# Two head attentions with VectorE in another order and the normalisation cut in pieces; a gated expert layer with a 128-row spreading product and its splits ahead of the router

## What is computed

```python
scores = einsum(q, k) * inv_sqrt_d + mask          # layer 0, softmax, times v
topv, topi = top_k(softmax(t @ gate_w.T), 6)       # layer 2
cw = zeros((T, 16)).at[rows, topi].add(topv / sum(topv))
routed = einsum('eti,edi,te->td', silu(g) * u, ed_w, cw)
```

## Time and profile before

| | |
|---|---|
| median of 3 runs | 4728.63 us (4726.76 to 4732.03) |
| profiled execution | 4728.14 us |
| its span, first to last instruction | 4726.4 us |
| mean granted TensorE clock | 0.937 of full |
| PE / DVE / ACT / POOL busy | 4134.5 (87%) / 2611.0 (55%) / 2047.8 (43%) / 888.4 (19%) us |

### The profile page before, as it was taken

How to read it: one execution, slowest core, us unless ns; L and a number is a source line. 1 busy time by engine, 2 the same in 40 slices (tenths; PEclk the granted TensorE clock), 3 DMA queues, 4 the chain that set the end, 5 groups by cost and what they waited for, 6 DMA issues and landing times. The chain is left out here.

```text
span 4726.4 us, 74274 instructions
## 1 busy us (share of the span) xinstructions
PE 4134.5 (87%) x25324; PEld 3338.8 (71%) x25324; DVE 2611.0 (55%) x5915; ACT 2047.8 (43%) x5270; POOL 888.4 (19%) x714
## 2 busy tenths in 40 slices
PE   5886999999896876999999996999979997887791
PEld 3554899999775764878877885777767775665671
DVE  5876998989475336444444443433333333776533
ACT  4775666666222433434333433333333332665140
POOL 1001333323000330000000000222212222000145
PEclk9987999999997997999999997999989999998596
DMA  2001000000001003000000001000010000000244
GB/s 62 14 14 46 1 0 0 0 0 1 25 20 43 1 29 111 8 6 6 6 6 6 6 5 57 13 5 9 5 53 10 9 10 21 14 11 25 89 135 129
DMA packets 100269, 119.29 MB, mean 25 GB/s; under 512 B 13777, under 2 KB 81201, under 8 KB 99761
## 3 DMA queue, kind: packets, MB, share of 16 engines
q1 hardware_dynamic: 93152, 97.25, 6.5%
q0 software_dynamic: 6864, 18.75, 1.4%
HBM read 93.03 MB, written 22.94 MB: 25 GB/s over the span
## 5 line engine op out<-in xcount | busy, mean ns | idle before, releaser
L1145 ACT ACTIVATE peer_tab<-peer_sims 128x128 f32<-128x128 f32 x1024 | 305.6, 392 | 0.0
L1152 POOL TENSOR_TENSOR peer_tab<-peer_sims 128x2048 f32<-128x2048 f32 x64 | 244.7, 3843 | 289.9 <-ACT peer_sims L1129 260.7
L1200 DVE SCALAR_TENSOR_TENSOR peer_tab<-peer_tab,peer_th 128x2048 f32<-128x2048 f32 x128 | 294.9, 2345 | 0.3
L1217 PE MATMUL bank<-ident,peer_tab 128*128 128x128 f32 x2048 | 246.9, 274 | 20.0 <-DVE peer_tab L1200 20.0
L1217 PEld LDWEIGHTS bank<-ident,peer_tab 128*128 128x128 f32 x2048 | 233.7, 142 | 33.6 <-DVE peer_tab L1200 21.2
L1627 DVE COPY mha_ks<-bank 128x512 f32<-128x512 f32 x128 | 88.5, 691 | 302.0 <-PE bank L1592 299.5
L1267 PE MATMUL bank<-peer_wd,peer_hh 128*128 128x256 f32 x1024 | 242.1, 380 | 1.8 <-DVE peer_hh L1258 1.8
L1732 PE MATMUL bank<-mha_wo,mha_oT 128*128 128x256 f32 x1024 | 242.9, 380 | 0.0
L1240 PE MATMUL bank<-peer_hT,peer_wg 128*128 128x256 f32 x1024 | 241.9, 379 | 0.0
L643 DVE TENSOR_TENSOR moe2a_b<-moe2a_a,bank 128x512 f32<-128x512 f32 x104 | 71.5, 687 | 296.5 <-PE bank L556 273.7
L643 DVE TENSOR_TENSOR moe2b_b<-moe2b_a,bank 128x512 f32<-128x512 f32 x96 | 66.0, 687 | 273.3 <-PE bank L556 252.2
(11 more groups left out here) (518 smaller groups left out, 11105.8 us busy)
## 6 DMA issues: line engine op xcount, KB each, us to landing
m_y_rows<-moe_y SPq DMA_DIRECT2D x79, 128.0 KB, 1.7
att_ctxT<-in_ctxT_dram SPq DMA_DIRECT2D x32, 256.0 KB, 2.7
x<-in_x_dram SPq DMA_DIRECT2D x4, 1024.0 KB, 9.6
lin_ctxT<-in_ctxT_dram SPq DMA_DIRECT2D x16, 256.0 KB, 2.7
mem_ctxT<-in_ctxT_dram SPq DMA_DIRECT2D x16, 256.0 KB, 2.8
mem_ctx<-in_ctx_dram SPq DMA_DIRECT2D x16, 256.0 KB, 3.1
t_scratch<-mha_hTf SPq DMA_DIRECT2D x8, 512.0 KB, 4.8
moe2a_hTf<-t_scratch SPq DMA_DIRECT2D x8, 512.0 KB, 3.7
```

Source lines behind the costliest of these rows:

```text
L1145: i = nc.scalar.activation(tab[g][h][:, b * P:(b + 1) * P], sims[:, g, h, P:2 * P], ACT.Identity, bias=sims[:, g, h, b:b + 1])
L1152: nc.gpsimd.tensor_tensor(out=tab[g][h][:].rearrange("p (a b) -> p a b", b=P), in0=sims[:, g, h, P:2 * P].unsqueeze(1).broadcast_to([P, NB ...
L1200: nc.vector.scalar_tensor_tensor(out=tab[g][h][:], in0=tab[g][h][:], scalar=th[:, g, h:h + 1], in1=tab[g][h][:], op0=ALU.is_ge, op1=ALU.mu ...
L1217: i = nc.tensor.matmul(TB[n % 2][:, j * P:(j + 1) * P], tab[g][h][:, blk * P:(blk + 1) * P], core.ident[:], start=(j == 0 and h == 0), sto ...
```

## The change

In both head attentions VectorE's turn becomes one written-out order: residual of (t-2, 1), maxima of (t, 0), statistics of t+2, result of (t-1, 0), (layer 3: half of the spread keys, `square_dve`), result of (t-1, 1), residual of (t-1, 0), maxima of (t, 1), (layer 3: `neg_dve`), the rows of t+2, and the spread keys. `norm_dve` is cut into `stats_dve`, `square_dve` and `rows_dve`.

In the quantised stage `queries_dve` goes; ScalarE scales the queries by row (`queries_act`), and the scale by column and the bias are added when the transposed queries are copied (`q_copy`, two pieces). The mask is split into a high part (`mask_act`, ScalarE) and a rest (`mask_pool`, GpSimd), and the mask product becomes two fp32r products instead of one fp32 product. `columns_pe` and `columns_act` prepare the columns once.

In the expert layer `sel` and `cwT` get 128 rows, the lower 64 of them zero, so that the spreading product is a 128-row one. At the stage's start the splits of gate and up weights come ahead of the router, those of the down weights behind it, and TensorE waits for each only where it needs it.

```diff
-        sel, gw = sb("sel", [64, H], FP32R), sb("gw", [P, C, E])
+        sel, gw = sb("sel", [P, H], FP32R), sb("gw", [P, C, E])
...
-        cwTf, cwT_hi, cwT = sb("cwTf", [64, TILE]), sb("cwT_hi", [64, TILE], FP32R), sb("cwT", [64, 2, TILE], FP32R)
-        e_ready, cw_done, cw_zeroed, cw_init, cwTf_ready = sem("e_ready"), sem("cw_done"), sem("cw_zeroed"), sem("cw_init"), sem("cwTf_ready")
+        cwTf, cwT_hi, cwT = sb("cwTf", [64, TILE]), sb("cwT_hi", [64, TILE], FP32R), sb("cwT", [P, 2, TILE], FP32R)
+        e_ready, cw_done, cw_zeroed, cw_init, cwT_ready = sem("e_ready"), sem("cw_done"), sem("cw_zeroed"), sem("cw_init"), sem("cwT_ready")
+        sel_zeroed = sem("sel_zeroed")
...
+            act.wait_ge(cwT_ready, t)
         nc.scalar.activation(cwT[0:32, par, :], F[0:32, :], ACT.Copy)
+        if isinstance(t, int) and t < 2:
+            nc.scalar.activation(cwT[64:P, par, :], F[64:P, :], ACT.Copy)
...
-            pe.wait_ge(w_lo_made, (j // QB + 1) * (len(raws) - 1))
-            pe.wait_ge(w_hi_made, (j // QB + 1) * len(raws))
+            pe.wait_ge(w_lo_made, (j // QB) * (len(raws) - 1) + 2 * C)
+            pe.wait_ge(w_hi_made, (j // QB) * len(raws) + 2 * C)
...
+            if j == 0:
+                pe.wait_ge(cwT_ready, t + 1)
+            if is_first(t) and j % QB == 0:
+                pe.wait_ge(w_lo_made, (j // QB + 1) * (len(raws) - 1))
+                pe.wait_ge(w_hi_made, (j // QB + 1) * len(raws))
             nc.tensor.matmul(CW[:], sel[:, j * P:(j + 1) * P], cwT[:, par, :], start=True, stop=True).then_inc(cw_ready, 1)
...
-            nc.vector.tensor_tensor(out=cwT[32:64, par, :], in0=cwTf[32:64, :], in1=cwT_hi[32:64, :], op=ALU.subtract)
         nc.vector.tensor_tensor(out=hTs[1][:, par, :, :], in0=hTf[:], in1=hTs[0][:, par, :, :],
                                 op=ALU.subtract).then_inc(hT_ready, 1)
+
+    def low_weights_dve(dve, t, par):
+        dve.wait_ge(f_emptied, (t + 1) * NF)
+        nc.vector.tensor_tensor(out=cwT[32:64, par, :], in0=cwTf[32:64, :], in1=cwT_hi[32:64, :], op=ALU.subtract).then_inc(cwT_ready, 1)
...
+                low_weights_dve(dve, t, par)
             low_dve(dve, t, par)
...
+                raw = raws[2 * C + 1][:, 0:raw.shape[1]]
+                act.wait_ge(sel_zeroed, 1)
...
+    GATE_UP, DOWN = slice(0, 2 * C), slice(2 * C, None)
...
+                loaded_act(act, 0, 0)
+                split_act(act, 0, GATE_UP)
+                router_act(act, 0)
+                cwT_act(act, 0, 0)
+                split_act(act, 0, DOWN)
...
+                low_dve(dve, 0, 0)
+                split_dve(dve, 0, GATE_UP)
+                router_dve(dve, 0)
+                low_weights_dve(dve, 0, 0)
+                split_dve(dve, 0, DOWN)
...
+                nc.gpsimd.memset(raws[2 * C + 1][64:P, :], 0.0).then_inc(sel_zeroed, 1)
...
+        swq_col, bq_col = sb("swq_col", [P, C]), sb("bq_col", [P, C])
+        identr = sb("identr", [P, P], FP32R)
+        mask_hi = [sb(f"mask_hi{i}", [P, GU, S], FP32R) for i in range(2)]
+        mask_lo = [sb(f"mask_lo{i}", [P, GU, S], FP32R) for i in range(2)]
...
-    def norm_dve(dve, t):
+    def stats_dve(dve, t):
...
         nc.vector.tensor_scalar(ve[:], mv[:, :, 1], LN_EPS, None, ALU.add).then_inc(var_ready, 1)
+
+    def square_dve(dve, t):
+        norm_chain.begin(t, 2)
         dve.wait_ge(rstd_ready, t + 1)
+        nc.vector.tensor_tensor(out=ms[:], in0=rstd[:], in1=rstd[:], op=ALU.mult).then_inc(norm_chain.sem, 1)
+        dve.wait_ge(norm_chain.sem, norm_chain.next())
+        nc.vector.tensor_tensor(out=ms[:], in0=ms[:], in1=mv[:, :, 1], op=ALU.mult).then_inc(ms_ready, 1)
+        norm_chain.end()
+
+    def rows_dve(dve, t):
         if quant:
+            norm_chain.begin(t, 2)
+            dve.wait_ge(rstd_ready, t + 1)
...
+                dve.wait_ge(qf_ready, t)
             nc.vector.tensor_reduce(out=sx[:], in_=xn[:], axis=AX.X, op=ALU.max, apply_absolute_value=True).then_inc(norm_chain.sem, 1)
...
+    def mask_act(act, t, par):
+        act.wait_ge(ctx_in[par], (t // 2 + 1) * n_ctx)
+        if some((t - 1) * GU):
+            act.wait_ge(scored, (t - 1) * GU)
+        nc.scalar.activation(mask_hi[par][:], mask[par][:], ACT.Copy).then_inc(hi_ready, 1)
+
+    def mask_pool(pool, t, par):
+        pool.wait_ge(hi_ready, t + 1)
+        if some((t - 1) * GU):
+            pool.wait_ge(scored, (t - 1) * GU)
+        nc.gpsimd.tensor_tensor(out=mask_lo[par][:], in0=mask[par][:], in1=mask_hi[par][:], op=ALU.subtract).then_inc(lo_ready, 1)
+
+    def queries_act(act, t):
+        fwait_filled(act, t, QUERIES)
         if some((t - 1) * 3 + LAST // 2 + 1):
-            dve.wait_ge(filled[LAST % 2], (t - 1) * 3 + LAST // 2 + 1)
-        F = FB[QUERIES % 2]
+            act.wait_ge(filled[LAST % 2], (t - 1) * 3 + LAST // 2 + 1)
         for g in range(GU):
-            i = nc.vector.scalar_tensor_tensor(out=qf[:, g, :], in0=F[:, g * D:(g + 1) * D], scalar=sx[:, g:g + 1], in1=swq[:],
-                                               op0=ALU.mult, op1=ALU.mult)
-        i.then_inc(q_chain.sem, 1)
-        dve.wait_ge(q_chain.sem, q_chain.next())
-        dve.sem_inc(emptied[QUERIES % 2], 1)
-        nc.vector.tensor_tensor(out=qf[:], in0=qf[:], in1=bq[:].unsqueeze(1).broadcast_to([P, GU, D]), op=ALU.add).then_inc(qf_ready, 1)
+            i = nc.scalar.activation(qf[:, g, :], FB[QUERIES % 2][:, g * D:(g + 1) * D], ACT.Copy, scale=sx[:, g:g + 1])
+        i.then_inc(qf_ready, 1)
+        act.wait_ge(qf_ready, t + 1)
+        act.sem_inc(emptied[QUERIES % 2], 1)
...
+                i = nc.scalar.activation(qT[par][:, c, :], FB[k % 2][:, c * UNIT:(c + 1) * UNIT], ACT.Identity,
+                                         bias=bq_col[:, c:c + 1], scale=swq_col[:, c:c + 1])
+            i.then_inc(emptied[k % 2], 1)
+            return
...
+                pe.wait_ge(lo_ready, t + 1)
             for c in range(C):
-                nc.tensor.matmul(SB[g][c][:].rearrange("p (h k) -> p h k", k=S), core.ident[:],
-                                 mask[par][:, g, :].unsqueeze(1).broadcast_to([P, H8, S]), start=True, stop=False, skip_group_check=True)
+                for n, part in enumerate((mask_hi, mask_lo)):
+                    nc.tensor.matmul(SB[g][c][:].rearrange("p (h k) -> p h k", k=S), identr[:],
+                                     part[par][:, g, :].unsqueeze(1).broadcast_to([P, H8, S]), start=(n == 0), stop=False, skip_group_check=True)
...
+        if not quant and some(n):
+            dve.wait_ge(on_ready, n)
...
                 keys_act(act, t + 1)
+                if quant:
+                    queries_act(act, t + 1)
...
+            if g == 1 and quant and exists(t + 1):
+                mask_act(act, t + 1, nxt)
             if g == 1 and exists(t + 1):
                 values_act(act, t + 1, nxt, 0)
...
-            (t1, p1, g1), (t2, p2, g2), (t3, p3, g3) = (back(t, par, g, k) for k in (1, 2, 3))
-            if exists(t):
-                max_dve(dve, t, par, g)
-            if exists(t3):
-                residual_dve(dve, t3, p3, g3)
-            if g == 0 and quant and exists(t + 1):
-                queries_dve(dve, t + 1)
-            if g == 0 and not quant and exists(t + 1):
-                spread_dve(dve, t + 1, nxt, KM_DVE[0:1])
-            if exists(t1):
-                result_dve(dve, t1, p1, g1)
-            if g == 0 and quant and exists(t + 1):
-                spread_dve(dve, t + 1, nxt, KM_DVE)
-            if g == 1 and not quant and exists(t + 1):
-                spread_dve(dve, t + 1, nxt, KM_DVE[1:2])
-            if g == 1 and not quant and exists(t + 1):
-                neg_dve(dve, t + 1, nxt)
-            if g == 1 and exists(t + 2):
-                norm_dve(dve, t + 2)
+        if exists(t - 2):
+            residual_dve(dve, t - 2, par, 1)
+        if exists(t):
+            max_dve(dve, t, par, 0)
+        if exists(t + 2):
+            stats_dve(dve, t + 2)
+        if exists(t - 1):
+            result_dve(dve, t - 1, nxt, 0)
+        if not quant and exists(t + 1):
+            spread_dve(dve, t + 1, nxt, KM_DVE[0:1])
+        if not quant and exists(t + 2):
+            square_dve(dve, t + 2)
+        if exists(t - 1):
+            result_dve(dve, t - 1, nxt, 1)
+            residual_dve(dve, t - 1, nxt, 0)
+        if exists(t):
+            max_dve(dve, t, par, 1)
+        if not quant and exists(t + 1):
+            neg_dve(dve, t + 1, nxt)
+        if exists(t + 2):
+            rows_dve(dve, t + 2)
+        if exists(t + 1):
+            spread_dve(dve, t + 1, nxt, KM_DVE if quant else KM_DVE[1:2])
 
     def unit_gp(pool, t, par):
         if quant and exists(t + 1):
+            mask_pool(pool, t + 1, 1 - par)
             bias_pool(pool, t + 1)
         if exists(t + 2):
             norm_pool(pool, t + 2)
```

74 lines of the change are left out of this document (44 added, 30 removed).

## The result

The changed kernel takes 4888.5 us in the median of 4 runs (4884.3 to 4893.5), against 4730.3 us for the kernel before on the same chip: a ratio of 1.033, 95% interval 1.0317 to 1.0342. The forecast was 4817 us with a range of 4745 to 4895. The direction and the mechanism are as predicted; all three stages came out somewhat worse than their term, 71 us in all. The profiled execution of the changed kernel spans 4885.6 us.

A forecast was written before the change was run, and what follows sets the result against it. Both attentions were taken as bound by a ring of waits, the expert layer by the spacing of TensorE's instructions. Terms 124 + 44 - 78 - 2 = +88 us gave 4817 us, range 4745 to 4895.

The forecast's parts named there:

- Steps 1 and 2: Quantised attention's turn: scores and output product, 2.2 us, then VectorE's residual, maxima, statistics and first result, to 9.0 us.
- the ring: Quantised attention: chain of waits going once around per turn, TensorE, VectorE, TensorE, ScalarE, GpSimd, VectorE; 29.1 us, 31.0 with slow scores.
- The clock term: Quantised attention: TensorE idles over 7 us before the first scores, which at 1.2 GHz take 1.9 us more.
- Step 3: Quantised attention's turn, TensorE: result transposes 0.2 us, mask product 0.92, second scores to transposes 3.17; ends at 13.3.
- the quantised term: Quantised attention: 8.2 us more per turn, 98 us over twelve full turns, with start and end turns +124 (100 to 160).
- Steps 4 to 6: Quantised attention's turn: ScalarE to 20.5 us, GpSimd's mask rest, bias and 1/std to 23.1, VectorE's rows and spread to 29.1.
- the first rival: Quantised attention: GpSimd does not hold VectorE up; turn 20.8 us, -24 us in all, 4669 us in total; chance 0.13.
- The other attention: Non-quantised attention: residual at the turn's head delays the second maxima; 3.2 us a turn thirteen times, +44 us (15 to 55).
- The expert layer: Spreading product loses 0.39 us of shape cost 200 times, -78, in full as nothing else nears its limit; with splits -80.
- The 64-row product's cost stays: Expert layer rival: the wait the product carries, not its shape, costs the time; 78 us not won, 4895 us; chance 0.05.
- More of both attentions at half clock: Rival: upper ends of both attention terms, as TensorE will be idle twice a turn; 4864 us; chance 0.08.
- Low parts late in every block: Expert layer rival: GpSimd's longest subtraction makes the low part 0.15 us late every block; +30 us, 4847 us; chance 0.02.

## Why the prediction was right, and where it was too small

- **Steps 1 and 2 of the ring** (residual waited for, first result): 10.9 us with the slow scores by the forecast, 290.83 - 280.36 = 10.5 measured in the turn shown, 10.3 to 11.2 in all eleven of the window and 10.9 in their mean. The clock term of 1.9 us is nearly right: first scores of 3.3 to 3.7 us in every steady turn, 1.3 to 1.7 more than before.
- **Step 3** (result transposes, mask, scores, to ScalarE's copy) is the step that was too small: 4.3 us by the forecast, 298.06 - 290.83 = 7.2 in the turn shown, 4.4 to 7.2 over the eleven turns and 6.1 in their mean. In the turn shown the mask product took 292.96 - 290.98 = 1.98 us and not 0.92, the second scores 3.68 and not 1.94. In the two turns whose second scores took 1.94 us the step took 4.37 us, the forecast's figure, and those turns took 31.4 and 31.7 us against 31.0. So the chain was sized rightly and the clock was not: the forecast had kept "the second scores run slow as well", 2.8 us, for its upper end, because 2.4 us of idle is less than the 3.04 of the earlier trace rows. That makes 1.8 of the 2.0 us between 31.0 and 33.0 us a turn, and most of the 27 us by which the quantised term (+124) missed (+151).
- **Steps 4 to 6** (ScalarE, GpSimd, VectorE): 7.2, 2.6 and 6.0 us by the forecast; 7.3 (298.06 to 305.38), 2.6 (to 307.97) and 6.1 (to 314.11) measured. The idle time forecast at about 7 us is 8.35.
- **That GpSimd's queue is the cause** was argued from one profile and is now shown, by undoing it alone from either side (-113 and -136 us by the ratios). The second of these is the condition of the first rival, "if the mask's high part were made early enough"; its ring of 20.8 us was 24.7, and its 4669 us were 4754. With the spread ahead of the rows the turn is 21.5 and the first scores run at full clock, so the rows in the ring, and the slow scores with them, were what that rival had left out.
- **The other attention**: +44 forecast, 55 to 59 measured. The second maxima begin 13.4 us after the scores (13.25 forecast) in every second turn, and 14.4 in the others, where the scores took 2.8 to 2.9 us. The gate product takes 3.6 to 3.8 us against 2.0, where 1.2 of the possible 1.9 were taken. From the maxima to the gate product it is 8.05 us in every turn, some 0.35 less than before, where the forecast had no change. In the mean 13.9 + 8.05 + 3.6 = 25.5, and not 24.7: here too the size of the clock's part was off, and the path was right as far as the timeline shows.
- **The expert layer**: -80 forecast, -58 in the trace and -54 to -70 timed. The price of the shape was right, 0.366 us a block for 0.39. In the last tile, which has no router work beside it, the twelve distances gave 57.5 - 53.1 = 4.4 us back, in full. The step that failed is "nothing else is near its limit here". In the other tiles the router's work on VectorE and ScalarE's table loads made a low part late (0.85 us of idle on TensorE, released by GpSimd's subtraction), in a block that before had little or no such wait. Such a tile gave 3.4 us for 4.8, 19 us in 14 tiles. Most of it, 1.1 us a tile, is the block of 5.54 us, and its subtraction did not lengthen: it took 1.28 us and came late because it started late. The other block, of 4.70 us, does hold the one long subtraction of each tile:

```profile
3267.78 2.32 POOL L639 TENSOR_TENSOR moe2a_hh_lo<-moe2a_hh,moe2a_hh_hi 128x512 fp32r<-128x512 f32 x1 [3.60 <-ACT moe2a_hh_hi L630]
```

  It ends at 3270.10 and the first down product starts at 3270.16, and the block is 0.27 us longer than an ordinary one; the prediction had weighed 0.15 us of lateness for it and set it at nothing. The ns min/median/max of all subtractions are these, for those of the earlier trace rows:

```profile
L639 POOL TENSOR_TENSOR moe2a_hh_lo<-moe2a_hh,moe2a_hh_hi x104: 1261/1288/2326, 3101.0 to 3583.4; 128x512 fp32r<-128x512 f32 x104
```

  The rule that the prediction weighed (the Trainium skill, SBUF — State Buffer, section "SBUF: two separate sides") has VectorE and GpSimd exclude each other on a shared port while a VectorE operation with two SBUF inputs runs. By it the prediction left the long case with a few operations of a tile; median and maximum have not moved, and there is one long subtraction in each tile but the last, before and after, which agrees.
- **The splits ahead of the router**: -2 forecast for both stages, about -4 in the trace. From TensorE's last instruction of the stage before, the first spreading product came 5.5 and 5.7 us earlier in the two stages, but the third only 2.5 and 3.2, of which 0.7 each is the pitch of two blocks. The second one waits for VectorE's product of the first block, 6.47 us against 2.56 in the lines of the result. That product needs ScalarE, which first splits the next weights and stood idle 3.44 us for their transfer (at 3095.29). This is what the prediction said: the second block still waits for ScalarE's split of the next weights.
- **The rivals.** "The 64-row product's cost stays" is out. "More of both attentions at half clock" (4864) had the right mechanism and too low a chance. "Low parts late in every block" happens in two of the thirteen blocks of a tile.

The three large misses, 27, 15 and 22 us, have one sign and one reason: each term was sized with the clock and the slack of the kernel before, and the change takes both away. With the 7 us outside the three stages they are the 71 us. They add up and do not cancel, so the direction is no luck; but the top of the range, 4895, is only 6 us above the measurement.

## What to carry to other kernels

Before an instruction with a late input is put first in the queue of an idle engine, list what stands behind it there: 17 us of idle time a turn did not keep one 0.45 us subtraction from costing 8 us, and the same subtraction behind another late wait cost 35 us in all. When a step is saved on the bounding engine in every pass of a loop, look for the passes in which another chain was within that saving of being late. In a ring of waits, moving a step pays only if it crosses the point where the ring leaves the engine; list the ring first and see which side it lands on.
